# Self-attention of a decoder layer: the output projection as three products of split operands, values' and output weights streamed through two buffers

## The reference, cut to what matters

```python
h = x * rsqrt(mean(x * x)) * norm_w
q, k, v = h @ w_q, h @ w_k, h @ w_v                       # 512 -> 16 heads of 64
ll = where(causal, q @ k.T * scale, NEG)                  # local logits
scores = h @ scorer_w + scorer_b
_, idx = top_k(scores, 128)                               # 128 keys seen a second time
lg = where(idx <= pos, q @ k[idx].T * scale, NEG)
attn = softmax(concatenate([ll, lg], axis=-1))
o = attn[..., :W] @ v + attn[..., W:] @ v[idx]
x1 = x + o @ w_out                                        # (512 x 1024) @ (1024 x 512)
```

## Time and profile before

| | |
|---|---|
| median of 3 runs | 2158.5 us |
| profiled execution | 2162.13 us, span 2160.2 us |
| mean granted clock | 0.926 |
| TensorE busy | 1954.8 us (90%) |
| VectorE, ScalarE, GpSimd busy | 1288.1, 986.0, 953.1 us |
| self-attention | 0 to about 1425 us |
| DMA | 154.10 MB, 71 GB/s over the span |

### The profile page before, as it was taken

The page is one execution under the profiler, slowest core; times in us unless marked ns, Lnnn a source line. Parts: engine busy times, 40 slices in busy tenths (PEclk is TensorE's granted clock), DMA queues, the critical chain, the costliest instruction groups (busy, mean ns, idle before and its releaser), DMA issues. The chain is left out here.

```text
span 2160.2 us, 34587 instructions
## 1 busy us (share of the span) xinstructions
PE 1954.8 (90%) x10377; PEld 1476.6 (68%) x10377; DVE 1288.1 (60%) x3621; ACT 986.0 (46%) x2487; POOL 953.1 (44%) x1900
## 2 busy tenths in 40 slices
PE   3699999999999999999999999768999999878998
PEld 3577677667667767757757767537888888854665
DVE  5476476467557557557647646416887878646400
ACT  2455345446446535535535635417555656313310
POOL 2354454454454455454445444426665656320000
PEclk9899999999999999999999999879887878669999
DMA  6612121211221211121121111030124111150000
GB/s 202 246 59 83 54 80 45 86 69 59 84 75 59 80 59 67 63 88 59 71 70 67 60 69 69 1 102 27 40 63 139 62 62 62 52 202 0 1 10 10
DMA packets 60099, 154.10 MB, mean 71 GB/s; under 512 B 11347, under 2 KB 12371, under 8 KB 51336
## 3 DMA queue, kind: packets, MB, share of 16 engines
q1 hardware_dynamic: 59272, 149.78, 19.9%
q0 software_dynamic: 640, 2.10, 0.3%
HBM read 125.64 MB, written 26.21 MB: 70 GB/s over the span
## 5 line engine op out<-in xcount | busy, mean ns | idle before, releaser
L479 POOL TENSOR_TENSOR units<-units,fixed 128x1 f32<-128x1 f32 (+1 forms) x384 | 233.7, 609 | 645.6 <-ACT probs L544 645.4
L544 ACT ACTIVATE probs<-probs,units 128x512 f32<-128x512 f32 (+3 forms) x512 | 284.9, 557 | 492.8 <-DVE units L654 492.8
L662 DVE TENSOR_TENSOR pt_lo<-pt_bank,pt_hi 128x512 fp32r<-128x512 f32 (+2 forms) x384 | 222.8, 599 | 183.7 <-ACT pt_hi L554 182.9
L484 POOL TENSOR_SCALAR probs<-probs,units 128x512 f32<-128x512 f32 (+3 forms) x512 | 278.0, 550 | 0.0
L786 PE MATMUL pt_bank<-ident,probs 128*128 128x128 f32 x1280 | 189.9, 286 | 60.1 <-POOL probs L484 56.2
L654 DVE CUSTOM_DVE_ANT_0 probs<-s_bank,bias 128x512 f32<-128x512 f32 (+3 forms) x512 | 227.0, 487 | 13.3 <-issue 13.1
L761 PE MATMUL pj_bank<-ht_hi,wqk 128*128 128x512 f32 x512 | 220.4, 430 | 9.6 <-DMA wqk<-wqk_split 8.0
L843 PE MATMUL pj_bank<-w_o,o_t 128*128 128x512 f32 x512 | 225.7, 592 | 1.4 <-DVE o_t L667 1.4
L762 PE MATMUL pj_bank<-ht_hi,wqk 128*128 128x512 f32 x512 | 207.1, 404 | 0.0
L763 PE MATMUL pj_bank<-ht_lo,wqk 128*128 128x512 f32 x512 | 207.0, 404 | 0.0
L786 PEld LDWEIGHTS pt_bank<-ident,probs 128*128 128x128 f32 x1280 | 139.9, 144 | 96.7 <-issue 61.2
(11 more groups left out here) (258 smaller groups left out, 3952.9 us busy)
## 6 DMA issues: line engine op xcount, KB each, us to landing
wqk<-wqk_split SPq DMA_DIRECT2D x63, 1024.0 KB, 4.8
xt<-x SPq DMA_DIRECT2D x36, 256.0 KB, 2.8
xb<-in_x SPq DMA_DIRECT2D x8, 1024.0 KB, 7.9
wqk_split<-w_stage SPq DMA_DIRECT2D x16, 512.0 KB, 6.0
xr<-in_x SPq DMA_DIRECT2D x32, 256.0 KB, 4.4
x<-xr SPq DMA_DIRECT2D x32, 256.0 KB, 2.1
am<-in_L_ffn_attention_mask SPq DMA_DIRECT2D x8, 1024.0 KB, 5.4
out<-x SPq DMA_DIRECT2D x32, 256.0 KB, 2.1
```

The source lines that it names most:

```text
L479: nc.gpsimd.tensor_tensor(rden[:, slot, 0:k], den[:, slot, 0:k], minus[:, 0:k], ALU.pow).then_inc(rden_ready, 1)
L484: ins = nc.gpsimd.tensor_scalar(probs[:, slot, c0:c0 + nk], probs[:, slot, c0:c0 + nk], rden[:, slot, k:k + 1], 1.0, ALU.mult, ALU.mult)
L544: ins = nc.scalar.activation(probs[:, slot, c0:c0 + nk], probs[:, slot, c0:c0 + nk], ACT.Exp, bias=nmax[:, slot, k:k + 1], scale=-1.0, acc ...
L662: nc.vector.tensor_tensor(dst, src, hi.bitcast(F32), ALU.subtract).then_inc(pt_taken, 1)
```

## The change

- The output projection multiplies split operands: `o_hi`, `o_lo` by `wo_hi`, `wo_lo`, three fp32r products in place of one plain fp32 product.
- `ot` writes `o_sum` (plain fp32, where the raw weights lay); a new kind `oh`, one a pair, rounds it to `o_hi` (ScalarE) and subtracts to `o_lo` (VectorE). It stands last in the slot of the pair's `ot`.
- Two buffers `wide` (2 MB each) take turns with value weights (a half of the width, hi and lo) and output weights (`wide[1]` holds `wo_hi`, `wide[0]` `wo_lo`). Value weights are stored to `wv_split` once, output weights to `wo_split`; a new kind `load` fetches 2 MB four times a batch, in slots 12, 7, 24 and 16 (loads 0 to 3).
- Output weights are split in the first period: splits 6 and 7 at the ends of slots 3 and 4, with their loads and stores.
- `PIECES` moves: v3b to the slot 23 of v3a, k1b from slot 1 to slot 0, v4a to v7a one slot later, v7b to the end of slot 15. Slot 1 has no piece.

```diff
-PIECES = {0: "v3b k1a", 1: "k1b", 2: "q2a q2b o0a- o0b-", 3: "k2a k2b o1a- o1b-", 4: "o2a-", 5: "o2b- o3a-",
-          6: "o3b- q3a q3b", 7: "k3a k3b", 8: "q4a q4b v4a", 9: "v4b k4a k4b", 10: "v5a", 11: "v5b q5a q5b",
-          12: "k5a k5b v6a", 13: "v6b", 14: "q6a q6b v7a", 15: "v7b k6a k6b", 17: "q7a q7b k7a",
+PIECES = {0: "k1a k1b", 2: "q2a q2b o0a- o0b-", 3: "k2a k2b o1a- o1b-", 4: "o2a-", 5: "o2b- o3a-",
+          6: "o3b- q3a q3b", 7: "k3a k3b", 8: "q4a q4b", 9: "k4a k4b v4a", 10: "v4b", 11: "q5a q5b v5a",
+          12: "v5b k5a k5b", 13: "v6a", 14: "v6b q6a q6b", 15: "k6a k6b v7a v7b", 17: "q7a q7b k7a",
           18: "k7b ht0+ ht1+ ht2+ ht3+", 19: "v0a+ v0b+", 20: "q0a+ q0b+ v1a+ v1b+", 21: "k0a+ k0b+ v2a+",
-          22: "v2b+", 23: "q1a+ q1b+ v3a+"}
+          22: "v2b+", 23: "q1a+ q1b+ v3a+ v3b+"}
@@ attention_plan
+        at.append(("oh", p, 3 * p + 4 if p else 6))
+    at += [("load", k, (-12, 7, 24, 16)[k]) for k in range(4)]
@@ buffers
-        wv_hi, wv_lo = sb("wv_hi", [P, DC, H * HD], F32R), sb("wv_lo", [P, DC, H * HD], F32R)
+        wide = [sb(f"wide{i}", [P, 2, DC, D], F32R) for i in range(2)]
+        wo_hi, wo_lo = (wide[i].rearrange("p w c d -> p (w c) d") for i in (1, 0))
-        W_ORDER = [("v", 0), ("q", 0), ("k", 0), ("v", 1), ("q", 1), ("k", 1)]
+        W_ORDER = [("v", 0), ("q", 0), ("k", 0), ("v", 1), ("q", 1), ("k", 1), ("o", 0), ("o", 1)]
-        SPLIT_IN_SLOT = {0: 3, 1: 4, 2: 5}
+        SPLIT_IN_SLOT = {0: 3, 1: 4, 2: 5, 3: 6, 4: 7}
@@ SyncE
+            def store_values(hw):
+                sp.wait_ge(split_lo, SPLIT_BEFORE[3 * hw + 1])
+                sp.dma_start(wv_split[hw], wide[hw][:, :, :, :]...).then_inc(wv_stored, 16)
...
+                if kind == "load":
...
+                    sp.wait_ge(pj_ready, last)
+                    sp.dma_start(wide[to][:, :, :, :]...,
+                                 (wv_split[0], wv_split[1], wo_split[1], wo_split[0])[i]).then_inc(wide_in[to], 16)
...
             def weights_left(slot):
                 if slot == 0:
                     load_weights(5)
-                if slot == 1:
-                    for half_ in range(2):
-                        store_split(4, half_)
-                if slot == 2:
+                    store_values(1)
+                if 1 <= slot <= 4:
                     for half_ in range(2):
-                        store_split(5, half_)
-                    sp.wait_ge(split_lo, SPLIT_BEFORE[6])
-                    sp.dma_start(w_o[:, :, :], ...).then_inc(small_in, 16)
+                        store_split(3 + slot, half_)
+                    if slot < 3:
+                        load_weights(5 + slot)
@@ ScalarE
+                if kind == "oh":
+                    act.wait_ge(o_taken, n.count(2 * NPAIR, 2 * i + 2))
+                    nc.scalar.copy(o_hi[:, i, :], o_sum[:, i, :]).then_inc(o_hi_ready, 1)
@@ VectorE
+                if kind == "oh":
+                    dv.wait_ge(o_hi_ready, n.count(NPAIR, i + 1))
+                    nc.vector.tensor_tensor(o_lo[:, i, :], o_sum[:, i, :], o_hi[:, i, :].bitcast(F32),
+                                            ALU.subtract).then_inc(o_lo_ready, 1)
@@ TensorE
-                        ins = nc.tensor.matmul(to[:, :], o_t[:, c, P * i:P * i + P], w_o[:, c, :],
-                                               start=(c == 0), stop=(c == NPAIR - 1))
+                        ins = product(to[:, :], o_hi[:, c, P * i:P * i + P], o_lo[:, c, P * i:P * i + P],
+                                      wo_hi[:, c, :], wo_lo[:, c, :], c == 0, c == NPAIR - 1)
```

More of the change, by code:

```diff
@@ L319, in self_attention, with split_views @@
         x1_rows = x1.rearrange("b (t p) d -> b p t d", p=P)
-        w_dram = {n: w.rearrange("(c p) e -> p c e", p=P) for n, w in (("q", w_q), ("k", w_k), ("v", w_v))}
+        w_dram = {n: w.rearrange("(c p) e -> p c e", p=P) for n, w in (("q", w_q), ("k", w_k), ("v", w_v), ("o", w_out))}
         def pairs_of(tile):
             return tile.rearrange("p c (j e) -> p j c e", j=2)
+        def split_views(i, half_, part):
+            if W_ORDER[i][0] == "o":
+                return (stage[:, half_, part].rearrange("p j c e -> p (j c e)"),
+                        raw[:, i % 2, 2 * half_:2 * half_ + 2, :].rearrange("p c d -> p (c d)"))
+            return stage[:, half_, part], pairs_of(raw[:, i % 2, :, 256 * half_:256 * half_ + 256])
         def in_pairs(tile, u, bank_):
@@ L360, in store_split @@
                 sp.wait_ge(split_lo, SPLIT_BEFORE[i] + half_ + 1)
+                if n == "o":
+                    at = (2 * hw + half_) * 2 * DC * P
+                    for w in range(2):
+                        sp.dma_start(wo_split[w, :, at:at + 2 * DC * P],
+                                     stage[:, half_, w].bitcast(F32).rearrange("p j c e -> p (j c e)")
+                                     ).then_inc(staged[half_], 16)
+                    return
                 for j in range(2):
@@ L394, in work @@
                     load_pair(i)
+                if kind == "load":
+                    to = i % 2
+                    if i == 0:
+                        if n.fixed and n.index == 1:
+                            sp.wait_ge(wv_stored, 16)
+                            last = proj_ring.count(("v", TT - 1), Round(0, 0))
+                        else:
+                            last = proj_ring.count(("o", TT - 1), n.ahead(-2))
+                    elif i == 1:
+                        if n.fixed and n.index == 0:
+                            return
+                        if n.fixed and n.index == 1:
+                            sp.wait_ge(wv_stored, 32)
+                        last = proj_ring.count(("o", TT - 1), n.ahead(-1))
+                    elif i == 2:
+                        final = n.fixed and n.index == B - 1
+                        last = proj_ring.count(*((("k", NPAIR - 1), n) if final else (("v", TT - 1), n.ahead(1))))
+                    else:
+                        if n.fixed and n.index == 0:
+                            for half_ in range(2):
+                                sp.wait_ge(staged[half_], 192)
+                        last = proj_ring.count(("v", 2 * TT - 1), n)
+                    sp.wait_ge(pj_ready, last)
+                    sp.dma_start(wide[to][:, :, :, :].bitcast(F32).rearrange("p w c d -> p (w c d)"),
+                                 (wv_split[0], wv_split[1], wo_split[1], wo_split[0])[i]).then_inc(wide_in[to], 16)
                 if kind == "xr":
@@ L581, in _ @@
             work("qb", 1, zero)
-            tail = ("ht",) + tuple(k for k in PIECE_KINDS)
+            work("vb", 3, zero)
+            tail = ("ht", "oh")
             mixed = [a for s in range(NG) for a in act_order(s, tail)]
@@ L876, in _ @@
             work("tw", 0, zero)
-            for kind, i in (("qa", 1), ("qb", 1), ("va", 3)):
+            for kind, i in (("qa", 1), ("qb", 1), ("va", 3), ("vb", 3)):
                 work(kind, i, zero)
@@ L885, in act_order @@
     woven = (("m", 0), ("t", 0), ("m", 1), ("t", 1), ("ot", 0), ("ot", 1))
-    order = engine_order(spread if slot % 3 == 1 else woven, PIECE_KINDS, ("ht",))
+    order = engine_order(spread if slot % 3 == 1 else woven, PIECE_KINDS, tail)
     return [a for a in order if a[3] == slot]
```

76 lines of the change are left out of this document (45 added, 31 removed).

## The result

The kernel after takes **2220.5 us** (median of 6 runs, 2219.0 to 2228.4), the kernel before 2160.3 us on the same chip (2157.6 to 2161.4): ratio **1.0294**, 95% interval 1.0279 to 1.0310, 60 us slower. The forecast was 2173 with a range of 2140 to 2192: the sign was right, the time lies outside the range.

The account below looks back on a forecast made before the run. The kernel was taken to be paced by TensorE (busy 161.8 of 169.5 us in a batch). Terms -48 + 22 + 2.5 + 8.5 + 13 + 2 + 4 = +4, with the clock +14.5, on 2158.5 gave 2173 us, range 2140 to 2192.

Parts of the forecast that it names:

- Output products: Output projection on TensorE: 256 fp32 products become 256 x 3 split products, -48 us (bounds -45 and -49).
- oh: Rounding and subtraction delay VectorE's next m, exposed in slots 12, 15, 16 and 18: +22 us (bounds 14 and 28).
- Loop boundary: Slots 23, 0, 1: VectorE's 2.7 us stop stays, v3b ends later; +0.8 at five changes, net +2.5 us (-3 to +5).
- The loads of wide: The 2 MB weight loads have 13 us or more until use: 0; at worst under 1 us a batch.
- GpSimd: Slots 6 and 7: oh's subtractions delay GpSimd's statistics, for which TensorE waits: +8.5 us (bounds 0 and 8.5).
- The sentence on two SBUF operands: From the Trainium skill: a VectorE instruction with two SBUF inputs and a GpSimd SBUF read exclude each other for a whole instruction.
- First batch: Two more splits at the ends of slots 3 and 4 wait for stores, making m(5) late: +13 us (7 to 18).
- Clock: New gaps at slot 17 to 18 and slot 1 make TensorE's clock fall six times: +10.5 us (bounds 0 and 32).
- Rivals 1: The waits appear, but the clock does not fall and GpSimd is not held: 2154 us, chance 0.22.
- rival 2: VectorE's lateness is absorbed and the first batch's splits are cheap: -25 us, 2133.5 us, chance 0.22.
- rival 3: The clock falls at nearly every new gap and for longer: 2190 us, chance 0.10.
- rival 4: The loads of wide come late, each batch held some us at o0a or v0a: 2180 us or more, chance 0.03.

Follow-up runs that it names:

- a_ohlater: Kernel after with oh moved one slot on, except the last two, which stay in slots 22 and 25: 2198.0 us, ratio 1.0172 to the kernel before.
- a_piecesback: Kernel after with the pieces' order of the kernel before, so load 2 is issued behind the jump: 2174.2 us, ratio 1.0058 to the kernel before.
- a_load2late: Kernel after with load 2 waiting for k(1), the last piece of slot 0, behind xr and xb: 2194.3 us, ratio 1.0175 to the kernel before.
- b_plus2mb: Kernel before with one more 2 MB transfer a batch (not behind the last), in slot 24 ahead of xr: 2196.2 us against 2155.5, ratio 1.0186.
- b_pad12: Kernel before with twelve tiny memsets on VectorE at the very start: 2169.0 us against 2155.3, ratio 1.0043.

## Why the prediction was wrong

**Output products: right.** -45.8 against -48, in bounds.

**oh: right.** Each slot was foreseen from the order of VectorE and the slack in the earlier trace rows: +25.8 against +22, or 0.95, 0.76, 0.48 and 1.02 us a batch against 0.75, 0.6, 0.28 and 1.15. a_ohlater shows that the place is the cause, for slot 12 least. That slots 19 and 22 would be covered by the fuller slots 20 and 23 held too; a_piecesback, without the fuller slot 23, is 0.7 us longer in slot 0.

**Loop boundary: the step that failed.** The prediction read the earlier trace rows as "VectorE is still for 2.7 us behind its last instruction" and carried the 2.7 us over as a fixed length, so that only v3b's later end counted, +0.8 a time. "This stays" is the sentence that failed: 2.7 us became 5.5 to 5.8, and a second stop of 4.1 to 4.3 followed. It had the load 2 that starts there, but priced it in another step only ("The loads of wide", 0), by the room until its own use, and not by what else needs DMA at that moment. Measured is +9.5 a time, +46.1 in all against +2.5: 43.6 of the 47.5 us by which 2173 was short. By the runs: with load 2 behind the jump (a_load2late) it is about +4 (0.8 as reckoned, some 1.4 of second stop; the rest is not taken apart, and TensorE's clock is 0.69 in the 5 us behind it), and the load adds 5.5.

**GpSimd: right in kind**, 0.98 us a batch against 1.2, and +5.8 in six batches (the seventh is the first batch, in its own row) against 8.5 in seven. The sentence on two SBUF operands held, with small instructions: 0.20 became 0.74.

**First batch: under-sized**, +18 against +13, at the upper bound. The chain of splits was the right mechanism (8.6 us go with the last two); the values' stores count 4. The other 5 us stay open.

**Clock.** The size was near, the places were not, so that it was near is luck. There was no fall at the eight gaps of 1.81 to 1.93 us before slot 18's transposes (1.00 in the 4 us behind 548.67), but one at each of the five jumps (0.50 from 600 to 604), behind waits of 8 us that the forecast had not, and one in the last batch's slot 9 behind a gap of 1.93 (0.50 from 1363 to 1366). Slot 1 is 1.8 us longer at a jump, against the kernel before, than at the changes without one, and slot 9's +3.5 is that gap and 1.6 more: 10.7 in all against 10.5.

**Rivals.** Rivals 1 and 2 were out with the forecast; rival 3 (2190, more falls of the clock) had no fall that it named, except at the jumps; rival 4 made load 2 late for its own use: it landed 7.9 us after its issue, 16 us before its first use at 611.5. What happened was none of them, and the range's end of 2192 left it out. At the other end the range began at 2140, above rival 2's own 2133.5, which had a chance of 0.22.

## What to carry to other kernels

A loop's jump back can be a fetch through the DMA engines: let no large transfer be in flight at it. Here 2 MB issued 0.7 or 1.0 us ahead of VectorE's branch cost 5.5 and 6.4 us a jump by the profiles, and issued 3.8 or 6.2 us behind it they held nothing up; what lies between was not tried. Test a suspected one by adding its bytes to the old kernel, once at that moment and once some microseconds later. When the profile says "issue" for an idle engine, count its instructions: a stop that stays at a number, not at an operation, is the program's layout, and a few idle instructions ahead of the loop move it. A short operation added to an in-order engine should stand behind the one that the next stage waits for; moved one slot on it gave 26 us back here.

## What was not expected of the hardware

- A jump costs VectorE 2.5 to 2.95 us with no data in flight, 5.5 to 5.8 in the kernel after and 6.7 to 7.0 in b_plus2mb, with 2 MB issued 1.3 and 1.6 us ahead of its last instruction's end. Why b_plus2mb's is the longest stays open.
- The same kernel is 0.43% slower (0.25 to 0.61%) with twelve memsets of 0.06 us at its start.
- Short waits don't tell by their size whether the clock falls. In b_pad12 TensorE waits three times in slots 0 and 1 of each jump. With 0.42, 1.01 and 0.85 us, and with 0.55, 0.60 and 0.85, the granted clock stays at 1.00 and the sixteen pv products take 2.8 us; with 0.54, 0.77 and 0.85, with 0.55, 0.89 and 0.86, and with 0.55, 0.69 and 0.86 it is 0.57 to 0.61 and they take 4.2 to 4.3. That is the whole difference of that kernel's slot 1 (0.05 or 1.65 to 1.9 us longer than before).
